# Graph attention and three GNN layers on one core: the output product of the attention stage a graph later and in the scores' bank, a running minimum in place of a maximum and its negation, GpSimd's masks in pieces of 128 columns

## The reference, cut to what matters

```
q = heads(x @ Wq);  k = heads(x @ Wk);  v = heads(x @ Wv)
scores = einsum('bhnd,bhmd->bhnm', q, k) / sqrt(32)
scores = where(adj, scores, -inf)
attn = softmax(scores, axis=-1)
out = einsum('bhnm,bhmd->bhnd', attn, v)            # back to (b, n, 256)
x = layernorm(x + relu(out) @ Wo)
```

## Time and profile before

| | us |
|---|---|
| median of three runs (1756.13 to 1760.15) | 1758.32 |
| the profiled execution, its own time | 1757.66 |
| its span, first to last instruction | 1755.9 |
| attention stage in it, up to the last statistics | about 433 |
| busy in the span: PE, DVE, ACT, POOL | 1631.8, 1372.9, 1246.0, 1232.0 |
| mean granted clock of PE, share of full speed | 0.977 |

### The profile page before, as it was taken

How to read it: one execution, slowest core, us unless ns; L and a number is a source line. 1 busy time by engine, 2 the same in 40 slices (tenths; PEclk the granted TensorE clock), 3 DMA queues, 4 the chain that set the end, 5 groups by cost and what they waited for, 6 DMA issues and landing times.

```text
span 1755.9 us, 40514 instructions
## 1 busy us (share of the span) xinstructions
PE 1631.8 (93%) x12032; PEld 1441.2 (82%) x12032; DVE 1372.9 (78%) x5392; ACT 1246.0 (71%) x2884; POOL 1232.0 (70%) x2087
## 2 busy tenths in 40 slices
PE   4999999996599999999989999999999999999994
PEld 3877777774499899899979899899888888888894
DVE  2888888887678878787777877788787888888862
ACT  2888888885477767767757777767766777777763
POOL 3354445543368777777868778777868999999996
PEclk8999999998699999999999999999999999999997
DMA  6132223322212212212213122212211222222211
GB/s 195 50 96 83 78 78 96 96 77 74 81 40 96 96 36 72 72 37 70 72 36 96 61 70 72 72 36 72 72 36 61 70 74 72 73 94 72 73 49 48
DMA packets 152118, 127.41 MB, mean 73 GB/s; under 512 B 16512, under 2 KB 145024, under 8 KB 152064
## 3 DMA queue, kind: packets, MB, share of 16 engines
q1 hardware_dynamic: 145024, 124.30, 22.5%
q10 hardware_dynamic: 7040, 2.51, 0.6%
HBM read 89.04 MB, written 37.75 MB: 72 GB/s over the span
## 4 chain that ended last, share of the span: by engine, by line
PE 51%; POOL 16%; DVE 5%; issue 2%; ACT 1%; POOLq 0%; DVEq 0%; ACTq 0%
PE ps L45 22%; PE ps L879 22%; PE ps L852 3%; POOL xo L792 2%; POOL gnn_n L160 2%; POOL gnn_norm L786 2%; PE ps L866 2%; POOL gnn_norm L160 2%; POOL gnn_fin L805 2%; POOL inv L155 2%; DVE gnn_junk L1004 2%; PE ps L844 1%; POOL gnn_hb L775 1%; POOL gnn_hb L771 1%; PE ps L859 1%
## 5 line engine op out<-in xcount | busy, mean ns | idle before, releaser
L879 PE MATMUL ps<-gnn_w_hi,gnn_g_hi 128*128 128x256 f32 x1536 | 434.1, 283 | 0.0
L879 PE MATMUL ps<-gnn_w_lo,gnn_g_hi 128*128 128x256 f32 x1536 | 429.0, 279 | 0.0
L879 PE MATMUL ps<-gnn_w_hi,gnn_g_lo 128*128 128x256 f32 x1536 | 428.7, 279 | 0.0
L974 ACT ACTIVATE gnn_g_hi<-ps,b_cols 128x512 fp32r<-128x512 f32 x384 | 264.6, 689 | 206.9 <-PE ps L45 206.9
L45 PE MATMUL ps<-gnn_hT_hi,gnn_w_hi 128*128 128x512 f32 x768 | 339.5, 442 | 4.2 <-DVE gnn_g_lo L1075 4.2
L1075 DVE TENSOR_TENSOR gnn_g_lo<-ps,gnn_g_hi 128x512 fp32r<-128x512 f32 x384 | 262.7, 684 | 95.9 <-ACT ps L975 95.5
L45 PE MATMUL ps<-gnn_hT_hi,gnn_w_lo 128*128 128x512 f32 x768 | 304.0, 396 | 0.0
L45 PE MATMUL ps<-gnn_hT_lo,gnn_w_hi 128*128 128x512 f32 x768 | 303.8, 396 | 0.0
L879 PEld LDWEIGHTS ps<-gnn_w_lo,gnn_g_hi 128*128 128x128 f32 x1536 | 288.9, 188 | 2.2
L879 PEld LDWEIGHTS ps<-gnn_w_hi,gnn_g_hi 128*128 128x128 f32 x1536 | 288.8, 188 | 2.2
L879 PEld LDWEIGHTS ps<-gnn_w_hi,gnn_g_lo 128*128 128x128 f32 x1536 | 288.7, 188 | 0.0
(11 more groups left out here) (126 smaller groups left out, 3952.2 us busy)
## 6 DMA issues: line engine op xcount, KB each, us to landing
hist<-xo SPq DMA_DIRECT2D x48, 512.0 KB, 3.7
x<-hist SPq DMA_DIRECT2D x48, 512.0 KB, 3.8
aw<-in_L_gnn_attn_w SPq DMA_DIRECT2D x48, 256.0 KB, 4.1
gmask<-mask_hist SPq DMA_DIRECT2D x48, 256.0 KB, 4.0
att_xq<-in_x SPq DMA_DIRECT2D x16, 512.0 KB, 4.6
att_xl<-in_x SPq DMA_DIRECT2D x16, 512.0 KB, 3.7
gnn_fin<-hist SPq DMA_DIRECT2D x16, 512.0 KB, 3.9
out<-gnn_fin SPq DMA_DIRECT2D x16, 512.0 KB, 3.0
```

The source lines that it names most:

```text
L879: mm = e.matmul(FF2[j % 2], g[a][:, m, j * N:(j + 1) * N], V[b][:, m, :], start=(n == 0), stop=(n == len(terms) - 1))
L974: e.activation(g[0][:, m, :], FF1[FFB[m]], ACT.Gelu, bias=bias)
```

## The change

The output product of graph i-1 now stands in graph i's work on PE, between the second half projection and the transposes of the reciprocals. It is written to the first 256 columns of bank 0, part of S. So it waits until the masked scores of graph i+1 have been read (`scored`), and the scores of graph i+2 wait until its result has been read (`y_out`). The transposes of heads 0 to 3 wait for `att_out` of graph i-1 instead of `y_out`. On DVE the residual and the statistics of graph i-1 follow the copy L552 of graph i. The weights Wq are multiplied by minus the scale when they are split, masks are +1e30 instead of -1e30, the reduction keeps a minimum, and this is the exponents' bias as it is, with the exponential's scale -1; L530, `peak` and `peaked` are gone. On POOL, L298, L299 and L306 become four instructions of 128 columns each. PE's first pair of groups is written out too.

```diff
@@ POOL, make_masks
-                    e.tensor_scalar(mask[par][:], adjl[par][:], 0.0, MASKED, ALU.is_equal, ALU.mult).then_inc(masks_made, 1)
-                    e.tensor_scalar(adj_f[:], adjl[par][:], 1.0, None, ALU.mult).then_inc(eye_added, 1)
+                    for j in range(GROUP):
+                        ins = e.tensor_scalar(mask[par][:, j, :], adjl[par][:, j, :], 0.0, -MASKED, ALU.is_equal, ALU.mult)
+                    ins.then_inc(masks_made, 1)
+                    for j in range(GROUP):
+                        ins = e.tensor_scalar(adj_f[:, j, :], adjl[par][:, j, :], 1.0, None, ALU.mult)
+                    ins.then_inc(eye_added, 1)
...
-                    e.tensor_scalar(mask1[par][:], eye_sum[:], 0.0, MASKED, ALU.is_le, ALU.mult).then_inc(masks_made, 1)
+                    for j in range(GROUP):
+                        ins = e.tensor_scalar(mask1[par][:, j, :], eye_sum[:, j, :], 0.0, MASKED, ALU.is_le, ALU.mult)
+                    ins.then_inc(masks_made, 1)
@@ PE
+                def output_product(i, has2):
+
+                    if has2:
+                        e.wait_ge(scored, i + 3)
+                    e.wait_ge(y_out, START + i)
+                    e.wait_ge(attT_hi_out, i + 1)
+                    e.wait_ge(attT_lo_out, i + 1)
+                    split_product(e, WO, attT, (w_hi, w_lo), lambda x, k: x[:, k, :],
+                                  lambda w, k: w[:, 3, k, :]).then_inc(wo_made, 1)
...
                         e.wait_ge(exped, 2 * i + 2)
-                        e.wait_ge(y_out, START + i)
+                        e.wait_ge(att_out, START + i)
                         for h in range(4):
                             mm = e.transpose(PB[0][:, h * N:(h + 1) * N], probs[j % 2][:, h, :], ident[:])
                         mm.then_inc(pT_made, 1)
                         fill(t, par, j, 0, a1, a2, parts=(1,))
+                        if j or before:
+                            output_product(i - 1, has1)
                         e.wait_ge(pT_out_b, i + 1)
...
                         if has2:
                             e.wait_ge(scored, i + 2)
+                            e.wait_ge(y_out, START + i)
...
                             scores(i + 2, par2, j2)
                         fill(t, par, j, 1, a1, a2)
-                        e.wait_ge(attT_hi_out, i + 1)
-                        e.wait_ge(attT_lo_out, i + 1)
-                        split_product(e, PB[0][:, 0:D], attT, (w_hi, w_lo), lambda x, k: x[:, k, :],
-                                      lambda w, k: w[:, 3, k, :]).then_inc(wo_made, 1)
@@ ACT
-                                           scale=SCALE, accum_out=den[b][:, h:h + 1])
+                                           scale=-1.0, accum_out=den[b][:, h:h + 1])
...
-                            e.wait_ge(peaked, i + 2)
+                            e.wait_ge(scored, i + 2)
@@ DVE
+                    if n == 0:
+                        e.tensor_scalar(w_hi[:, 0], w_raw[:, 0], -SCALE, None, ALU.mult)
+                        e.tensor_copy(w_hi[:, 1], w_raw[:, 1]).then_inc(wa_split, 1)
+                        e.wait_ge(wa_split, 1)
+                        e.scalar_tensor_tensor(out=w_lo[:, 0], in0=w_raw[:, 0], scalar=-SCALE, in1=w_hi[:, 0].bitcast(F32),
+                                               op0=ALU.mult, op1=ALU.subtract)
+                        e.tensor_tensor(w_lo[:, 1], w_raw[:, 1], w_hi[:, 1].bitcast(F32), ALU.subtract).then_inc(wa_split, 1)
+                        return
...
-                                                     in1=mask[par][:, j, :], scale=1.0, scalar=LOWEST,
-                                                     op0=ALU.add, op1=ALU.max, accum_out=peak[j % 2][:, h:h + 1])
+                                                     in1=mask[par][:, j, :], scale=1.0, scalar=-LOWEST,
+                                                     op0=ALU.add, op1=ALU.min, accum_out=neg_peak[j % 2][:, h:h + 1])
                     ins.then_inc(scored, 1)
-                    if between and at == NH:
-                        between()
-                    e.wait_ge(scored, i + 1)
-                    e.tensor_scalar(neg_peak[j % 2][:], peak[j % 2][:], -SCALE, None, ALU.mult).then_inc(peaked, 1)
...
                         e.tensor_copy(probsT[:, 0:4, :].rearrange("p h n -> p (h n)"), PB[0]).then_inc(pT_out_a, 1)
-                        if j == 0 and before:
+                        if j:
+                            residual(q, i - 1, par, j - 1, before)
+                            statistics(i - 1, par, j - 1)
+                        elif before:
+                            residual(q + par - 1, i - 1, 1 - par, GROUP - 1, True)
                             statistics(i - 1, 1 - par, GROUP - 1)
```

More of the change, by code:

```diff
@@ L189, in gnn_kernel @@
             probsT = sb("probsT", [P, NH, N])
-            peak = [sb(f"peak{i}", [P, NH]) for i in range(2)]
             neg_peak = [sb(f"neg_peak{i}", [P, NH]) for i in range(2)]
@@ L202, in gnn_kernel @@
             x_ld = sems("x_ld_even", "x_ld_odd")
-            (masks_made, xT_made, xT_hi_out, xT_lo_out, proj_made, proj_out, s_made, scored, peaked, exped,
+            (masks_made, xT_made, xT_hi_out, xT_lo_out, proj_made, proj_out, s_made, scored, exped,
              pT_made, pT_out_b, pT_out_a, pv_made, den_inv, rden_out, rdenT_made, rdenT_out, att_out,
@@ L206, in gnn_kernel @@
                 "masks_made", "xT_made", "xT_hi_out", "xT_lo_out", "proj_made", "proj_out", "s_made", "scored",
-                "peaked", "exped", "pT_made", "pT_out_b", "pT_out_a", "pv_made", "den_inv", "rden_out",
+                "exped", "pT_made", "pT_out_b", "pT_out_a", "pv_made", "den_inv", "rden_out",
                 "rdenT_made", "rdenT_out", "att_out", "attT_hi_out", "attT_lo_out", "wo_made", "y_out", "bn_out",
@@ L211, in gnn_kernel @@
             S = ps[:, 0:4, 0:2 * N]
+            WO = ps[:, 0, 0:D]
             A = [ps[:, 4, :], ps[:, 5, :]]
@@ L316, in body @@
                         e.wait_ge(masks_made, 2 * (t + 1))
-                        e.wait_ge(peaked, GROUP * t + 1)
+                        e.wait_ge(scored, GROUP * t + 1)
                         make_masks(q + (par + 1) // 2, 1 - par, t + 1)
@@ L375, in fill, with body @@
                             transpose_x(t + 2, k)
-                def body(q, par, a1, a2):
+                def output_product(i, has2):
[6 more added lines that the diff above has]
+                                  lambda w, k: w[:, 3, k, :]).then_inc(wo_made, 1)
+                def body(q, par, a1, a2, before=True):
                     t = 2 * q + par
-                    for j, i, _, (has2, t2, par2, j2) in graphs(q, par, a1):
+                    for j, i, has1, (has2, t2, par2, j2) in graphs(q, par, a1):
                         e.wait_ge(exped, 2 * i + 1)
@@ L424, in _ @@
                 scores(1, 0, 1)
-                steps(e, body)
+                body(0, 0, True, True, before=False)
+                body(0, 1, True, True)
+                steps(e, body, first=1)
+                output_product(B - 1, False)
             @block.scalar
@@ L490, in _ @@
                     xT_hi(1, k)
-                e.wait_ge(peaked, 1)
+                e.wait_ge(scored, 1)
                 exps(0, 0, 0)
@@ L498, in _ @@
                 e.sem_inc(y_out, START)
+                e.sem_inc(att_out, START)
                 def split_weights(n):
@@ L511, in xT_lo, with masked_scores @@
                         e.tensor_tensor(xT[1][:, k, :], A[k], xT[0][:, k, :].bitcast(F32), ALU.subtract).then_inc(xT_lo_out, 1)
-                def masked_scores(i, t_, par, j, between=None, at=NH):
+                def masked_scores(i, t_, par, j):
                     if j == 0:
@@ L540, in statistics, with residual @@
                         ins.then_inc(mv_out, 1)
+                def residual(q, i, par, j, before):
+                    if j == 0:
+                        if before:
+                            e.wait_ge(ln_out, START + 2 * q + par - 1)
+                        e.wait_ge(x_ld[par], 32 * (q + 1))
+                    e.wait_ge(wo_made, i + 1)
+                    e.tensor_tensor(y[par][:, j, :], WO, xl[par][:, j, :], ALU.add).then_inc(y_out, 1)
                 def body(q, par, a1, a2, before=True):
@@ L561, in body @@
                                                in1=rdenT[:].rearrange("p k n -> p (k n)"), op0=ALU.max, op1=ALU.mult).then_inc(att_out, 1)
-                        e.wait_ge(att_out, i + 1)
+                        e.wait_ge(att_out, START + i + 1)
                         e.tensor_copy(attT[0][:], att[:]).then_inc(attT_hi_out, 1)
@@ L565, in body @@
                         e.tensor_tensor(attT[1][:], att[:], attT[0][:].bitcast(F32), ALU.subtract).then_inc(attT_lo_out, 1)
[L566 to L573, removed]
-                        if has2:
[L577 to L581, removed]
+                        if has2:
```

(2 more changed lines are left out.)

2 lines of the change are left out of this document (removed).

## The result

The changed kernel takes 1738.6 us (median of four, 1738.0 to 1741.9) against 1759.2 before: a ratio of 0.9885, 95% interval 0.9873 to 0.9897, 20.6 us less where 16 were forecast (1741.7, range 1731 to 1751). A second series gave 1738.5 against 1758.3, 0.9882 (0.9865 to 0.9898).

What follows compares the result with a forecast made beforehand. PE, nearest to full, bounds the kernel, with ACT's exponentials limiting the group edge. A group takes 23.35 + 0.2 = 23.55 us against 24.4: 12.8 over fifteen, plus 3.5 in the last, taken as 16, gives 1741.7 us, range 1731 to 1751.

Steps and rivals of the forecast that it cites:

- Rival A: The forecast itself, chance 0.70: 11 to 21 us less, 1737 to 1747 us.
- 11.3 for the edge: Between two groups, j = 3 and j = 0 together last 4.7 + 6.6 us on PE; 12.1 before.
- the half of the stretching that was to remain: Per group, stretched instructions cost some 0.35 us before; 0.2 of it was taken to stay.
- The last group: No projections there, so DVE's 4.6 us sets the period: about 1.0 us less on three to four graphs, 3.5 us.
- PE's floor: PE's work without stops: 6.02 us for j = 0 to 2, 4.00 for j = 3, 22.1 a group.
- B: Rival, chance 0.08: ACT does not hold the group edge; 34 us less, 1724, or halfway, 1731.
- (a): Output product of graph i-1 waits for the masked scores of i+1; 1.4 us to spare at j = 1 or 2.
- (b): Scores of graph i+2 wait for the residual of i-1; 0.2 us to spare.
- DVE, late from L511, adds 0.15 to 0.2: At the group edge, DVE delays the output product and L401 of j = 0 by 0.15 to 0.2 us.
- L530 goes: off PE's path: Removing the negation, a slot of 0.12 us unstretched and 0.39 stretched, shortens DVE only.
- Masks in pieces: nothing for DVE: POOL's mask pieces priced at nothing for DVE, bounded by 0 and 0.35 us a group.
- The output product a graph later: PE's work stays 0.71 us; the 1.10 us stop at j = 3 goes, and residual and statistics fill DVE's 0.90 gap.

## Why the prediction was right, and where it was wrong

**The time and the sum.** 1741.7 forecast, 1738.6 measured, the faster side, within the range. Rival A as written. The steady group was right to 0.01 us, and that was luck. The forecast was 11.3 for the edge, 12.04 for two graphs, and 0.2 for the half of the stretching that was to remain. Measured are 11.46 for the edge and 12.1 for the two graphs: the 0.2 is there, but it is not stretching. With whole masks and the stretching back the pair is 47.15, 0.015 a group more. The old group's sum, from which the 0.35 for stretching came, has a slip as well: 12.1 + 12.04 is 24.14, not 24.05.

What is short is 4.6 us. The baseline was low: 24.4 a group was the mean from the first to the last graph, with the short last group in it; the steady group is 49.02 / 2 = 24.5, so fifteen groups gave 14.2 instead of 12.8. The last group gave less: 23.55 us from its first transposes to the last statistics before, 22.03 and 21.60 in two traces of the changed kernel, 1.5 and 2.0 of the 3.5 forecast. Its periods were to fall to DVE's 4.6; they went from 5.78, 5.75 and 5.58 to 5.84, 5.07 and 4.55, so only the last did. Together that is 16, as the sum had it and as the spans of the two profiled executions say (15.8; 17.7 with the second trace of the changed kernel). The 20.6 of the medians is 4 to 5 us more. The profiled execution of the changed kernel was the longest of its four; beyond that the difference stays open.

**PE's floor.** Right: 6.00 to 6.02 and 6.08 to 6.10 for the graphs without an edge, in the changed kernel and in all its variants but the one with the delayed residual. No B.

**The waits (a) and (b).** (a) held, except that at j = 0 the output product starts 0.14 after the last masked score, as the working had it at the edge. (b) held and was thin, as reckoned; what I had not reckoned is that a delay there costs more than itself at the edge, 0.55 for 0.34.

**The edge.** ScalarE's exponentials do hold the first transposes (0.85 us, once a group), and the 4.7 was 4.92. The fourth exponential is done at 182.64, 4.70 after 177.94, as forecast; the sum had left out what follows, the read of its sum (until 182.74, below) and 0.13 from there to L399 at 182.87.

```profile
182.55 0.19 ACT L467 ACTIVATION_READ_ACCUMULATOR att_probs<-att_probs,att_neg_peak 128x1 f32 x1
```

And I named one limit where there are two. "DVE, late from L511, adds 0.15 to 0.2" is the line that undersized it: take ScalarE's limit away and DVE adds 0.55 more.

**"L530 goes: off PE's path."** Wrong. Alone it gives 13.9 us. I had looked at a graph with j = 1, in which PE runs without a stop. In j = 0 and 2 it is DVE's chain, masked scores, negation, reciprocal, columns, that starts L395.

**"Masks in pieces: nothing for DVE."** Wrong as a price of the part, by 10.7 us in the old order; right as the price on top of the rest, 0.9 us between series and 0.03 us a pair. The bound of 0.35 a group was too low too: pieces alone took 0.53 a group. The step that failed is that stretched copies were counted as a loose remainder instead of being followed, one by one, to who waits for them.

**The output product a graph later.** I credited it with the stop of 1.10 us and the gap before L560. Both went, and the loop's rate shows nothing of it beside the small parts: the stop at j = 3 came back as a longer j = 0. It is worth 15.5 us alone and 2.9 us as the last part added.

**The port.** VectorE's copies and casts are stretched where work on GpSimd lies beside them, 0.40 to 0.46 us in 14 of them beside instructions of some 1.93 us in the kernel before. Beside a mask piece of some 0.65 us it is 0.1 at most in the loop of the kernel with pieces alone and of the changed one. The longest in the changed kernel, 578 ns for L578, does not lie beside a piece but beside the normalisation L160, which the change left as it was. The Trainium skill, "SBUF — State Buffer", section "Who interferes with whom", has the loser blocked for the whole instruction. The length, 0.46 beside 1.93, still disagrees. But what the prediction drew from that rule, that pieces would take the stretching away, is what the runs show, and my reading that a long one already lets it in "about where pieces would" is not. How the hold ends inside a long instruction stays open.

## What to carry to other kernels

Follow every stretched or tiny instruction on a nearly full engine to who waits for it, in every place of the loop and not in the one that runs smoothly. Parts that remove stops of the same chain do not add up: test them in pairs, for the cheap ones may already give all, and the large one then buys little. Where two engines close a stretch together, relieving one alone shows nothing, and both must be moved at once.

## What was not expected of the hardware

GpSimd's 128-column piece is not a quarter of the long instruction. The pieces of the last mask take 0.65 us each, and four of them with nothing beside them 2.76 from the first start to the last end (second line), against 1.93 us in one:

```profile
L311 POOL TENSOR_SCALAR att_mask<-att_eye_sum x64: 641/646/861, 19.3 to 390.8; 128x128 f32<-128x128 f32 x64
```

```profile
19.27 2.76 POOL L311 TENSOR_SCALAR att_mask<-att_eye_sum 128x128 f32<-128x128 f32 x4
```

(2.76 - 1.93) / 3 is 0.28 us for each further instruction. Here POOL's idle time hides it.
